# A two-layer graph network kernel on one core: x1 as one two-scalar operation late in VectorE's step, a spectrum copied earlier on ScalarE, and first loads in another order

## What is computed

```python
# layer 0
norm = (sum(adj, -1) + 1e-6) ** -0.5
f_hom = (adj @ ((x @ theta) * norm)) * norm
f_het = x @ W_h
gate = sigmoid(x @ W_t + b_t)
x = layernorm(x + elu(gate * f_hom + (1 - gate) * f_het))
# layer 1
h = relu(bn1(conv1(x)))                      # 1 tap
x_conv = relu(bn2(conv2(h)) + x)             # 17 taps along the nodes
s = x @ w_se.T + b_se
A = exp(-squared_distances(s)) * adj
x_nmp = A @ relu(x @ w_msg.T + b_msg)
gi = concat(x_conv, x_nmp) @ w_ih.T + b_ih   # three gates r, z, n
gh = x @ w_hh.T + b_hh
n = tanh(gi_n + sigmoid(gi_r + gh_r) * gh_n)
x = layernorm((1 - z) * n + z * x)
```

## Time and profile before

| | |
|---|---|
| runs of the kernel | 1990.43 us median of 3 (1988.78 to 1994.69) |
| the profiled execution's own time | 1989.04 us |
| its span, first to last instruction | 1986.9 us |
| mean granted TensorE clock | 0.98 |
| PE busy | 1887.1 us, 95% of the span |
| DVE busy | 1463.6 us, 74% |
| ACT busy | 1112.3 us, 56% |
| POOL busy | 422.3 us, 21% |

### The profile page before, as it was taken

The page is one execution under the profiler, slowest core; times in us unless marked ns, Lnnn a source line. Parts: engine busy times, 40 slices in busy tenths (PEclk is TensorE's granted clock), DMA queues, the critical chain, the costliest instruction groups (busy, mean ns, idle before and its releaser), DMA issues.

```text
span 1986.9 us, 35043 instructions
## 1 busy us (share of the span) xinstructions
PE 1887.1 (95%) x11046; PEld 1653.5 (83%) x11046; DVE 1463.6 (74%) x2972; ACT 1112.3 (56%) x2063; POOL 422.3 (21%) x378
## 2 busy tenths in 40 slices
PE   6999999996999899948999999999999999999997
PEld 6888888885999799947888888888888888888886
DVE  5889888886666788836777777777777777777774
ACT  6878888885666677734444444444444344444442
POOL 4666666664444200000000000000000000000000
PEclk9999999997999999978999999999999999999998
DMA  6777788875333598851212121212121212212200
GB/s 221 251 259 267 273 291 294 289 262 194 101 98 98 188 314 282 279 189 40 100 51 99 49 99 49 92 56 88 60 88 60 82 67 74 75 65 84 78 33 22
DMA packets 184169, 281.13 MB, mean 141 GB/s; under 512 B 14286, under 2 KB 126644, under 8 KB 179860
## 3 DMA queue, kind: packets, MB, share of 16 engines
q1 hardware_dynamic: 184084, 280.10, 41.9%
HBM read 178.60 MB, written 101.45 MB: 141 GB/s over the span
## 4 chain that ended last, share of the span: by engine, by line
PE 53%; issue 1%; DVE 1%; DMA 1%; SPq 0%; ACT 0%; POOLq 0%; POOL 0%; ACTq 0%; DVEq 0%
PE c_ps_g L1539 40%; PE c_ps_m L1517 5%; PE c_ps_m L1548 2%; PE c_ps_y L1574 1%; PE c_ps_m L1550 1%; PE c_ps_y L1632 1%; PE c_ps_m L1632 1%; PE c_ps_m L1549 1%; DMA c_yf<-y_spec 1%; PE c_ps_s L1617 0%; PE c_ps_y L1633 0%; PE c_ps_m L1633 0%; PE c_ps_g L1591 0%; PE c_ps_s L1588 0%; DVE c_wi_l L1482 0%
## 5 line engine op out<-in xcount | busy, mean ns | idle before, releaser
L1308 POOL TENSOR_TENSOR c_rstd<-c_var_eps,c_neg_half 128x4 f32<-128x4 f32 x32 | 32.3, 1008 | 1076.8 <-DVE c_var_eps L1446 1076.8
L1231 ACT ACTIVATE c_yo<-c_ps_y,c_shift,c_rstd 128x256 f32<-128x256 f32 x128 | 61.9, 564 | 169.5 <-DVE c_shift L1454 169.5
L1539 PE MATMUL c_ps_g<-c_ch,c_wi_l 128*128 128x512 f32 x384 | 154.5, 402 | 0.0
L1539 PE MATMUL c_ps_g<-c_nh,c_wi_l 128*128 128x512 f32 x384 | 153.2, 399 | 0.0
L1539 PE MATMUL c_ps_g<-c_xh,c_wh_l 128*128 128x512 f32 x384 | 152.0, 396 | 0.0
L1539 PE MATMUL c_ps_g<-c_xl,c_wh_h 128*128 128x512 f32 x384 | 151.9, 396 | 0.0
L1539 PE MATMUL c_ps_g<-c_ch,c_wi_h 128*128 128x512 f32 x384 | 151.6, 395 | 0.0
L1539 PE MATMUL c_ps_g<-c_xh,c_wh_h 128*128 128x512 f32 x384 | 151.6, 395 | 0.0
L1539 PE MATMUL c_ps_g<-c_cl,c_wi_h 128*128 128x512 f32 x384 | 151.5, 394 | 0.0
L1539 PE MATMUL c_ps_g<-c_nl,c_wi_h 128*128 128x512 f32 x384 | 151.1, 394 | 0.0
L1539 PE MATMUL c_ps_g<-c_nh,c_wi_h 128*128 128x512 f32 x384 | 150.8, 393 | 0.0
(11 more groups left out here) (219 smaller groups left out, 6187.9 us busy)
## 6 DMA issues: line engine op xcount, KB each, us to landing
w_spec<-a_spec SPq DMA_DIRECT2D x32, 1088.0 KB, 8.2
m_w<-w_spec SPq DMA_DIRECT2D x34, 1024.0 KB, 8.3
a_xt<-in_x_t SPq DMA_DIRECT2D x64, 256.0 KB, 3.3
a_xn<-in_x_n SPq DMA_DIRECT2D x64, 256.0 KB, 5.0
x_t<-a_x1t SPq DMA_DIRECT2D x64, 256.0 KB, 4.4
s_x<-x_t SPq DMA_DIRECT2D x64, 256.0 KB, 3.0
y_spec<-x_spec SPq DMA_DIRECT2D x64, 256.0 KB, 5.7
c_x<-x_t SPq DMA_DIRECT2D x32, 512.0 KB, 4.1
```

What stands on the lines that cost most here:

```text
L1231: nc.scalar.activation(yo[:, b], ps_y[:, b], ACT.Identity, bias=shift[:, b:b + 1], scale=rstd[:, b:b + 1]).then_inc(s_yo, 1)
L1308: nc.gpsimd.tensor_tensor(rstd[:, :], var_eps[:, :], neg_half[:, :], ALU.pow).then_inc(s_rstd, 1)
L1539: last = nc.tensor.matmul(out, stationary, moving, start=(count == 0), stop=(count == total - 1))
```

## The change

In layer 0:

- ACT copies the fourth spectrum ahead of `xh`, not behind it.
- DVE's `x1` becomes one `tensor_scalar` per graph with two numbers per partition (the mean and the reciprocal root), where it was a `scalar_tensor_tensor` whose third operand was the root, broadcast along the features. It and the variance's eps (`s_ve`) move to the end of DVE's step, behind `fl`, first `x1` and then `s_ve`.

In the GRU stage, for the first group alone:

- SP issues, behind `x1` of group 0, the message biases, `yf`, the convolution's tables and constants, `yr`, the adjacency and `xg` of group 0, and then the GRU's weights and biases; `x1` of group 1 comes behind them.
- ACT makes `di`, `dr_h` and `yh` of group 0 in the step of group 0's messages; `xs` waits there for `shift2`; the high parts of `wh` and `wi` come behind the similarities.
- DVE does `conv2_constants` and `yl` of group 0 behind `right_t`, and the GRU's bias sums and the low parts of `wh` and `wi` behind the first half of the convolution.
- PE waits for `di` and `dr` just before the inverse transform.

```diff
@@ layer 0, ACT
+                if ahead(7):
+                    spectra_out(t - 7, 3)
                 if live(1):
                     p = i - 1
                     r = (n - 1) % RING
                     reached(act, s_in[r], (k * (UNROLL // RING) + (n - 1) // RING + 1) * (16 * 2))
                     reached(act, s_gp, p - 1)
                     nc.scalar.activation(xh[:, v], xt[:, r], ACT.Copy).then_inc(s_xh, 1)
-                if ahead(7):
-                    spectra_out(t - 7, 3)
@@ layer 0, DVE: s_ve (L534) and x1 (L548) leave their places, and behind fl:
+                if live(6):
+                    reached(dve, s_root, p6 + 5)
+                    reached(dve, s_xp, p6 - 1)
+                    for b in range(2):
+                        last = nc.vector.tensor_scalar(x1[:, u, b], y[:, u, b], mv[:, u, b, 0:1], roots[:, u, 2 + b:3 + b], ALU.subtract, ALU.mult)
+                    last.then_inc(s_x1, 1)
+                if live(5):
+                    reached(dve, s_mv, p5 + 1)
+
+                    reached(dve, s_root, p5 + 3)
+                    nc.vector.scalar_tensor_tensor(sums_eps[:, v, 2:4], mv[:, v, :, 1], 1.0, eps[:, :], ALU.mult, ALU.add).then_inc(s_ve, 1)
@@ GRU stage, SP
+            def first_group():
+
+                for dst, src in ((bs_row[:, 0, :], b_se.partition_broadcast(P)), (bs_row[:, 1, :], b_se.partition_broadcast(P)),
+                                 (bm_row[:, 0, :], b_msg.partition_broadcast(P)), (bm_row[:, 1, :], b_msg.partition_broadcast(P))):
+                    sp.dma_start(dst, src).then_inc(s_b, 16)
+                y_of(0, 0)
+                for dst, src in ((di_raw[:, :], dft_i), (dr_raw[:, :], dft_r), (bn[:, :, :], bn2), (mk[:, :], masks), (fm[:, :], form)):
                     sp.dma_start(dst, src).then_inc(s_k2, 16)
+                y_rest_of(0, 0)
+                adjacency(0, 0)
+                x_again(0, 0)
+                sp.dma_start(wh_raw[:, :, :], w_hh).then_inc(s_wg[0], 16)
+                sp.dma_start(bi[:, :, :], b_ih).then_inc(s_wg[0], 16)
+                sp.dma_start(bh[:, :, :], b_hh).then_inc(s_wg[0], 16)
+                sp.dma_start(wi_raw[:, :, :], w_ih).then_inc(s_wg[1], 16)
@@ GRU stage, ACT
-                if isinstance(i, int) and i == 1:
-                    act.wait_ge(s_k2, 64)
-                    nc.scalar.activation(di[:, 0], di_raw[:, :], ACT.Copy).then_inc(s_dh, 1)
-                    nc.scalar.activation(dr_h[:, :], dr_raw[:, :], ACT.Copy).then_inc(s_dh, 1)
-                    act.wait_ge(s_n2c, 4)
-                if isinstance(i, int) and i == 2:
-                    act.wait_ge(s_wg[0], 16)
-                    nc.scalar.activation(wh_h[:, :, :], wh_raw[:, :, :], ACT.Copy).then_inc(s_wh, 1)
...
+                if first:
+                    act.wait_ge(s_k2, 80)
+                    nc.scalar.activation(di[:, 0], di_raw[:, :], ACT.Copy).then_inc(s_dh, 1)
+                    nc.scalar.activation(dr_h[:, :], dr_raw[:, :], ACT.Copy).then_inc(s_dh, 1)
+                    y_high(0, 0)
...
+                if first:
+                    act.wait_ge(s_n2c, 4)
+                    x_shifted(ga, v)
...
+                if first:
+                    act.wait_ge(s_wg[0], 48)
+                    nc.scalar.activation(wh_h[:, :, :], wh_raw[:, :, :], ACT.Copy).then_inc(s_wh, 1)
                     act.wait_ge(s_wg[1], 16)
                     nc.scalar.activation(wi_h[:, :, :], wi_raw[:, :, :], ACT.Copy).then_inc(s_wh, 1)
@@ GRU stage, DVE
-                if isinstance(i, int) and i == 1:
-                    conv2_constants()
-                if isinstance(i, int) and i == 2:
-                    constants()
-                    dve.wait_ge(s_wh, 2)
-                    nc.vector.tensor_tensor(wh_l[:, :, :], wh_raw[:, :, :], wh_h[:, :, :].bitcast(F32), ALU.subtract).then_inc(s_wl, 1)
+                first = isinstance(i, int) and i == 2
+                if first:
+                    dve.wait_ge(s_b, 64)
...
+                    if first:
+                        conv2_constants()
+                        y_low(0, 0)
...
+                if first:
+                    constants()
+                    dve.wait_ge(s_wh, 2)
+                    nc.vector.tensor_tensor(wh_l[:, :, :], wh_raw[:, :, :], wh_h[:, :, :].bitcast(F32), ALU.subtract).then_inc(s_wl, 1)
                     dve.wait_ge(s_wh, 3)
                     nc.vector.tensor_tensor(wi_l[:, :, :], wi_raw[:, :, :], wi_h[:, :, :].bitcast(F32), ALU.subtract).then_inc(s_wl, 1)
```

More of the change, by code:

```diff
@@ L543, in step @@
                                                    ALU.mult, ALU.add).then_inc(s_mix, 1)
-                if live(6):
-                    reached(dve, s_root, p6 + 5)
-                    reached(dve, s_xp, p6 - 1)
-                    for b in range(2):
-                        last = nc.vector.scalar_tensor_tensor(x1[:, u, b], y[:, u, b], mv[:, u, b, 0:1], roots[:, u, 2 + b:3 + b].to_broadcast([P, D]),
-                                                              ALU.subtract, ALU.mult)
-                    last.then_inc(s_x1, 1)
                 if live(2):
@@ new lines, in y_of, with y_rest_of, x_again @@
+            def y_of(g, v):
+                sp.dma_start(yf[:, v], y_spec[:, bass.ts(g, B)]).then_inc(s_yf[v], 16)
+            def y_rest_of(g, v):
+                for row, part in enumerate((0, 1, 0)):
+                    rows = slice(row * (RR // 3), (row + 1) * (RR // 3))
+                    sp.dma_start(yr[rows, v].bitcast(F32), y_rest[part, bass.ts(g, B)].rearrange("g d c -> (g d) c")).then_inc(s_yr[v], 16)
+            def x_again(g, u):
+                sp.dma_start(xg[:, u], x1_t[:, :, bass.ts(g, T)]).then_inc(s_xg[u], 16)
@@ L1210, in xconv_high, with x_shifted, y_high @@
                 nc.scalar.activation(ch[:, v, j], t2[:, j], ACT.Relu).then_inc(s_ch, 1)
+            def x_shifted(g, v):
+                loaded(act, s_xg, 1, g, v)
+                reached(act, s_t2, 2 * KD * g)
+                for j in range(KD):
+                    nc.scalar.activation(xs[:, j], xg[:, v, j], ACT.Identity, bias=shift2[:, j:j + 1]).then_inc(s_xs, 1)
+            def y_high(g, w):
+                loaded(act, s_yf, 1, g, w)
+                reached(act, s_inv, KD * g)
+                nc.scalar.activation(yh[:, :, :], yf[:, w], ACT.Copy).then_inc(s_yh, 1)
             def step(i, u, k, live):
@@ L1234, in step @@
                     n_tanh(gg, 0)
-                if live(2):
-                    loaded(act, s_xg, 1, ga, v)
-                    reached(act, s_t2, 2 * KD * ga)
-                    for j in range(KD):
-                        nc.scalar.activation(xs[:, j], xg[:, v, j], ACT.Identity, bias=shift2[:, j:j + 1]).then_inc(s_xs, 1)
+                if live(2) and not first:
+                    x_shifted(ga, v)
[4 more added lines that the diff above has]
+                    y_high(0, 0)
                 if live(2):
@@ L1281, in step @@
                     nc.scalar.activation(xh[:, w], x1[:, w], ACT.Copy).then_inc(s_xh, 1)
-                    loaded(act, s_yf, 1, g, w)
-                    reached(act, s_inv, KD * g)
-                    nc.scalar.activation(yh[:, :, :], yf[:, w], ACT.Copy).then_inc(s_yh, 1)
+                    if not (isinstance(i, int) and i == 1):
+                        y_high(g, w)
             pipeline(act, groups, 5, step)
@@ L1610, in step @@
                 if live(2):
+                    if isinstance(i, int) and i == 2:
+                        pe.wait_ge(s_dl, 2)
                     reached(pe, s_yl, ga + 1)
```

60 lines of the change are left out of this document (25 added, 35 removed).

## The result

The changed kernel takes 1958.94 us, the median of 4 runs (1956.62 to 1960.80), against 1991.47 for the kernel before, 4 runs beside it (1988.78 to 1994.69). The ratio is 0.9837, with a 95% interval of 0.9821 to 0.9853. The forecast was 1960.

A forecast was written before the change was run, and what follows sets the result against it. Layer 0 was held to be bound by a ring through ACT's copy order and PE, beside a slow GRU start. Gains of 22.0 + 7.5 = 29.5 us from 1989.0 gave 1959.5, stated as 1960; range 1952 to 1973.

The forecast's parts named there:

- The ring: Layer 0: tanh to tanh through ACT's copies, then PE's spectrum 0 to gate; 7.05 us a step, to become 6.69.
- step 65: Layer 0 step with no pair left to load, so no `xh` or `ah`; the copy follows `ex`, and it takes 6.69 us.
- 61 x 0.36 = 22.0: Layer 0: 61 steps stalled ahead of spectrum 0, each to lose 0.36 us, for a gain of 22.0 us.
- PE itself is full: Layer 0: below the 6.69 us step only PE's own passes are left between two tanhs, so no more gain was taken.
- None of this is on the ring ... I cost it at nothing: Layer 0: DVE's moves of `x1` and `s_ve` save 0.6 us of DVE work a step but count for no gain.
- without `s_ve` ahead of it `gd` is no later: Layer 0, DVE: `gd` ends no later than before, covering PE's earlier gate by 0.18 us or a little more.
- VectorE becomes the ring: Layer 0 rival: `x1` still meets `al`, taking 1.6 us; PE's gate waits for `gd`; 1971 to 1982 us; chance 16%.
- x1: Layer 0, DVE: in its new form behind `fl`, two graphs take 0.7 us, where it was 1.30.
- GpSimd's list becomes the ring: Layer 0 rival: POOL's operations behind `xh` make `al` late, step 0.25 us above 7.05; 8 us slower, 1997; chance 4%.
- The GRU part: GRU stage, first group: earlier loads and reordered work start the gates 7.0 to 8.3 us earlier, taken as 7.5.
- item 3: GRU first group: constants and `yl` enter the path after second messages of 2.9 us; `aa` comes 8.4 to 9.7 us earlier.
- The sum: Whole kernel: 22.0 + 7.5 = 29.5 us off the profiled 1989.0, giving 1959.5, stated as 1960.

The follow-up runs named there:

- e6: The changed kernel with one more small ACT copy (128x128, result unread) ahead of the fourth spectrum's copy; 1963.37 us in one run.
- e1: The kernel before with only ACT's copy of the fourth spectrum moved ahead of `xh`; 1989.47 us, ratio to before 0.9997.
- e2: The kernel before with only DVE's changes: `x1` as `tensor_scalar` behind `fl`, eps behind it; 1990.74 us, ratio to before 1.0004.
- e4: The changed kernel with `x1` still a `tensor_scalar`, but `x1` back ahead of `fl` and eps ahead of `gd`; 1979.63 us in one run.
- e3: The kernel before with only the GRU stage's first group changed, layer 0 as before; 1981.54 us, ratio to before 0.9957.
- f2: The kernel before with the copy ahead of `xh` and `x1` as `tensor_scalar` behind `fl`, eps in its old place; 1990.81 us in one run.
- f4: The kernel before with the copy ahead of `xh` and eps as a one-input `tensor_scalar` in its old place; 1991.11 us, ratio to before 1.0004.
- f1: The kernel before with the copy ahead of `xh` and eps at the step's end, `x1` in old form and place; 1977.41 us, ratio to before 0.9933.
- f3: Layer 0 of the changed kernel with `x1` in its old form in the new place, GRU stage of before; 1970.75 us in one run.
- e5: The changed kernel with ACT's `xh` moved behind the first `fh`; 2023.65 us in one run.
- g4: The changed kernel with eps directly behind the second `bn_aggr`, ahead of `diff`; 1959.68 us in one run.
- e7: The changed kernel with the first GRU group's weight parts and the sums' additions placed otherwise on ACT and DVE; 1955.48 us, ratio to before 0.9822.

## Why the prediction was right, and where its share-out was not

**The ring and its size: right, the last digit by luck.** A step of 6.69 was read from step 65, and 55 of the 63 steps after are 6.66 to 6.70. 61 x 0.36 = 22.0 is what the two tanhs show, 445.64 - 423.64. But the first four distances and the last were as short before, so 58 steps gain, by 0.38 in the median: a count too high and a size too low cancel. That "PE itself is full" below it is right to within some 0.03 us (e6).

**"None of this is on the ring ... I cost it at nothing": wrong.** This is the step that failed, for DVE's moves. By e1 the copy alone brings 0, by e2 the moves alone bring 0, and e4, the copy and x1's new form without the moves, is within 2 us of the GRU part alone (e3). The moves are a condition for all 22 us. The sentence on `gd` ahead of it ("without `s_ve` ahead of it `gd` is no later") was true, and it held the answer: I should have asked what `s_ve` would have done in its place, with `xl` moved by 0.4. The rows of the step in the kernel before showed it, DVE and then POOL:

```profile
309.59 0.32 DVE L534 SCALAR_TENSOR_TENSOR a_sums_eps<-a_mv,a_eps 128x2 f32<-128x2 f32 x1
```

```profile
308.61 1.29 POOL L423 TENSOR_TENSOR a_xl<-a_xt,a_xh 128x512 fp32r<-128x512 f32 x1 [0.55 <-ACT a_xh L351]
```

Eps took 0.32 for 128x2 numbers, and ended at 309.91, where `xl` ended (308.61 + 1.29 = 309.90). Had the diff held the copy alone, the same reasoning would have forecast 22 us and been wrong by 22.

**The rival "VectorE becomes the ring": did not come true, but its mechanism exists.** Its price, all of the 0.36 lost, is just what e1, f2 and f4 show, by eps on `xl` and not by x1 on `al`. The meeting of x1 and `al` is in f1: 1.49 and 0.93 us, and 8.9 of layer 0's 22.0 us lost.

**x1: size right, reason half right.** 0.7 was forecast, 0.73 measured. Of the 0.57 saved the new form gives 0.14 (f3), the place the rest. The 337 ns of the earlier trace rows say little of the form's rate by themselves; the slopes say more: `tensor_scalar` takes 284 ns at 128 columns and 337 at 256 in the kernel before, 0.4 ns a column, an operation of two SBUF tensors 405 at 256 and 675 at 512, 1.05 ns a column.

**The rival "GpSimd's list becomes the ring": did not come true; e5 made it so.** The forecast's cover of 0.3 for `al` is 0.27. The price was put at 0.25 a step above 7.05; once `xh` starts behind `hom`, it is 0.70 above.

**The GRU part: the order right, one term's size set by the clock.** Forecast were gates 36.5 behind the start and `aa` 23 to 24; the pair shows 35.34 and 22.17, a gain of 8.9 and not 7.5. The mis-sized term is in item 3: PE's second messages were priced at 2.9 us, like the first, and took 1.70 in the kernel after, at the upper of the two clock levels. The constants and `yl` took 3.5 (3.7 forecast), the stretch from `aa` 10.87 (10.9). The other kernels say how firm this is. All have the same passes behind the same gap of 0.93 us:

| second messages | kernels | `aa` | gates |
|---|---|---|---|
| granted clock 1.00 | after, e4, e5 | 22.2 to 22.7 | 35.34 to 35.83 |
| granted clock 0.50 | e3, e6, g4 | 23.3 to 23.6 | 36.45 to 36.72 |

Where the clock stayed low, the forecast is met. The kernels with the old GRU part fall into two sets in the same way: before, e1 and e2 have a clock of 0.90 in the mean between the second messages and `aa` and gates at 43.71 to 44.24, f1 to f4 have 0.50 there and gates at 45.34 to 45.97. So the 8.9 of the pair, and the 8.8 between the means of all old (44.9) and all new (36.1), hold some 1 us or more of clock. The nearest to like with like is before, e1 and e2 against e3, e6 and g4: 43.9 - 36.6 = 7.3.

**The sum: near, in part because terms missed in opposite directions.** 22.0 + 8.9 + 0.45 at the start is 31.4; the spans differ by 28.9. Some 2.4 us went between the last tanh and the GRU stage, most of it in the product stage, 198.65 us before and 200.78 after. The change touches nothing there. In twelve of the fourteen profiles this stage takes 198.2 to 199.6 us; only the kernel after and f3 are above 200.5, both at a mean granted clock of 0.98 and not 0.99. It is scatter between executions, which the forecast had not put into its range by itself. The forecast was also set from a median before of 1990.43, of three runs, where the four beside the kernel after have 1991.47. So the 1.1 us between 1960 and 1958.94 is closer than the terms were.

**What stays open.** Why a running POOL operation holds eps was not settled: by f1 and g4 the overlap is what counts, and by f4 one tensor input is enough, but no kernel tried other sizes of operands, or an `xl` of another form. Nor is it known why the clock rises in time for the second messages in some executions and not in others, with the same work ahead of it, and so whether the new order makes it likelier: it did in four of seven profiles with the new GRU part (e7 among them) and in none of seven with the old, where PE stands still for 11.3 us or more ahead of them.

## What to carry to other kernels

A gain read from a step that happens to lack one operation must be checked against everything that this operation's move drags along; here it pushed a POOL operation onto a 128x2 one on DVE, and of 22 us of gain 0.5 was left. When a tiny operation takes longer than others of its size, compare its end with the end of what runs on the other engine, and move it to where that engine is idle. A change that removes one wait by 0.36 us with covers of 0.14 and 0.27 around it is to be taken as a whole: e1, e4 and e5 are a line or two away from it, and each loses layer 0's gain or more. And where a stretch has gaps on PE, a single pair of profiles can differ by a clock level: compare the granted clock of the same passes before a gain is put down to the order.
